# An RWKV layer with a mixture of experts: row scaling and the second layer norm on VectorE, all squares on ScalarE

## What is computed

```python
xn = layernorm(x)
# s: one RWKV layer on xn
h  = ln(xn, ln1_w, ln1_b);  xk, xv, xr = mixes of h with h shifted by one token
k, v, r = xk @ att_kw, xv @ att_vw, xr @ att_rw
x2 = xn + (sigmoid(r) * wkv(decay, first, k, v)) @ att_ow     # wkv: a scan over tokens
h  = ln(x2, ln2_w, ln2_b);  xk, xr = mixes of h with h shifted by one token
kk = square(relu(xk @ f_kw))                                  # 512 wide
s  = x2 + sigmoid(xr @ f_rw) * (kk @ f_vw)
# g: a shared expert and one of 8 routed experts a token
shared = (silu(xn @ g) * (xn @ u)) @ d
score  = sigmoid(max of the router's logits)                  # one number a token
xs     = xn * score                                           # row scaling
routed = the chosen expert's (silu(xs @ g_e) * (xs @ u_e)) @ d_e
out = x + s * silu(shared + routed)
```

## Time and profile before

| what | value |
|---|---|
| runs | 555.39, 562.61, 565.73 us (median 562.61) |
| span of the profiled execution | 552.1 us, granted clock 0.977 |
| TensorE busy | 477.2 us, 86% of the span |
| VectorE busy | 401.3 us, 73% |
| ScalarE busy | 353.4 us, 64% |
| GpSimd busy | 279.0 us, 51% |
| DMA | 64.97 MB, mean 118 GB/s |

### The profile page before, as it was taken

One profiled execution on the slowest core, in us unless ns is written; L12 is line 12 of the kernel. 1 busy time (PEld: TensorE's weight loads), 2 busy tenths in 40 slices (PEclk: granted clock), 3 DMA queues, 4 the chain that ended last, 5 costly groups with the idle time before them and its releaser, 6 DMA issues. The chain is left out here.

```text
span 552.1 us, 9051 instructions
## 1 busy us (share of the span) xinstructions
PE 477.2 (86%) x2687; PEld 356.4 (65%) x2687; DVE 401.3 (73%) x808; ACT 353.4 (64%) x707; POOL 279.0 (51%) x329
## 2 busy tenths in 40 slices
PE   1989877879998789979898989898989898869796
PEld 1989444547575556569686868686868777644454
DVE  3553697858795877858696969797878788875345
ACT  4777424656663748576878686969696968554542
POOL 7565003565756375735273737363646464634440
PEclk9999898998999999989999999999999999999799
DMA  6339508210101010126363737373737372438395
GB/s 210 102 89 248 121 0 300 108 42 13 44 20 44 1 49 12 49 55 174 114 202 111 208 106 207 101 216 94 225 100 211 102 207 92 118 115 134 69 184 109
DMA packets 62592, 64.97 MB, mean 118 GB/s; under 512 B 5776, under 2 KB 50705, under 8 KB 62496
## 3 DMA queue, kind: packets, MB, share of 16 engines
q1 hardware_dynamic: 50736, 51.16, 32.5%
q0 software_dynamic: 10656, 11.68, 9.3%
q10 hardware_dynamic: 1152, 1.56, 0.9%
HBM read 46.86 MB, written 21.12 MB: 123 GB/s over the span
## 5 line engine op out<-in xcount | busy, mean ns | idle before, releaser
L857 POOL DMA_INDIRECT routed_out<-xh,xs x71 | 91.1, 1283 | 52.5 <-ACT xh L700 34.9
L849 POOL DMA_INDIRECT tokens_by_expert<-xn,pos x64 | 70.3, 1098 | 35.1 <-issue 18.5
L471 PE MATMUL bank_ring<-xh,ew 128*128 128x128 f32 x568 | 76.8, 279 | 0.0
L471 PEld LDWEIGHTS bank_ring<-xh,ew 128*128 128x128 f32 x568 | 70.8, 194 | 4.5 <-issue 3.8
L1090 DVE TENSOR_TENSOR kk<-rk 128x512 f32<-128x512 f32 x32 | 24.2, 755 | 61.2 <-ACT rk L658 55.6
L427 PE MATMUL bank_out<-fvw,kk 128*128 128x128 f32 x512 | 67.5, 278 | 0.0
L427 PEld LDWEIGHTS bank_out<-fvw,kk 128*128 128x128 f32 x512 | 63.4, 195 | 3.9 <-issue 3.9
L692 ACT ACTIVATE px<-bank_ring 128x256 f32<-128x256 f32 x71 | 27.1, 381 | 36.7 <-PE bank_ring L471 31.3
L831 POOL TENSOR_SCALAR x_sm<-x_mv 128x4 f32<-128x4 f32 x16 | 4.0, 247 | 81.4 <-DVE x_mv L1071 81.4
L485 PE MATMUL bank_ring<-ew,hx 128*128 128x128 f32 x284 | 43.5, 276 | 0.0
L387 PE MATMUL bank_fa<-xr,att 128*128 128x512 f32 x32 | 18.3, 656 | 24.6 <-ACT rk L658 23.8
(11 more groups left out here) (143 smaller groups left out, 1145.4 us busy)
## 6 DMA issues: line engine op xcount, KB each, us to landing
ew<-ex_w SPq DMA_DIRECT2D x71, 384.0 KB
xi<-x SPq DMA_DIRECT2D x20, 256.0 KB, 2.8
tokens_by_expert<-pad_row SPq DMA_DIRECT2D x1, 4686.0 KB, 20.4
xs<-tokens_by_expert SPq DMA_DIRECT2D x71, 66.0 KB
ew<-routed_out SPq DMA_DIRECT2D x16, 256.0 KB, 3.1
out<-xn POOLq DMA_DIRECT2D x12, 256.0 KB, 6.0
routed_out<-xh,xs POOLq DMA_INDIRECT x71, 2.9
tokens_by_expert<-xn,pos POOLq DMA_INDIRECT x64
```

Of the source, the lines that this page charges most:

```text
L471: last = nc.tensor.matmul(part(GU[n % 2], q, P), part(w, q, P), xt[:, 0:P], start=True, stop=True)
L849: nc.gpsimd.indirect_dma_start(xs_dram, bass.IndirectOffsetOnAxis(ap=POS[:, t:t + 1], axis=0), XN[:, t * XROW:(t + 1) * XROW], None).then_ ...
L857: nc.gpsimd.indirect_dma_start(routed_dram, bass.IndirectOffsetOnAxis(ap=XS[(n - 2) % NXS][:, CH:CH + 1].bitcast(i32), axis=0), XH[n % NXH ...
```

## The change

The row scaling (`scale_rows`, all 71 tiles) goes from ScalarE to VectorE as a tensor_scalar with one scalar a token. z2 (`make_z2`, 64 tiles) goes from ScalarE to VectorE as a tensor_scalar that subtracts the mean and multiplies by the inverse deviation, two scalars a token; it stands behind `wkv_b`. GpSimd loses the two small instructions that made the bias (L832, L837). All four squares of the channel mix are done by ScalarE; square 1 stands between relu 2 and relu 3, and relu 3 waits for it.

```diff
-                pe.wait_ge((s_kk, s_kd)[q % 2], 2 * c + 1 + q // 2)
+                pe.wait_ge(s_kk, 4 * c + q + 1)
 ...
# ScalarE
-            def make_z2(c):
-                act.wait_ge(s_nb2, c + 1)
-                if c > 0:
-                    act.wait_ge(s_z2t, c)
-                for j in range(TPC):
-                    nc.scalar.activation(part(Z2, j, P), part(X2[c % 2], j, P), ACT.Identity,
-                                         bias=SM2[:, 2 * TPC + j:2 * TPC + j + 1],
-                                         scale=SM2[:, TPC + j:TPC + j + 1]).then_inc(s_z2, 1)
 ...
                 if c > 0 or q >= 2:
-                    act.wait_ge((s_kk, s_kd)[q % 2], 2 * c + q // 2)
+                    act.wait_ge(s_kk, 4 * c + q - 1)
 ...
-            def scale_rows(n):
-                act.wait_ge(s_xs[n % NXS], 16 * (n // NXS + 1))
-                xs = XS[n % NXS]
-                nc.scalar.activation(xs[:, 0:CH], xs[:, 0:CH], ACT.Identity, scale=xs[:, CH + 1:CH + 2])\
-                  .then_inc(s_xsc, 1)
 ...
                 if C:
                     ffn_square(i - 1, 0)
                     ffn_relu(i - 1, 2)
+                    ffn_square(i - 1, 1)
                     ffn_relu(i - 1, 3)
                     ffn_square(i - 1, 2)
+                    ffn_square(i - 1, 3)
 ...
# GpSimd, rstd_of_x2
-                nc.gpsimd.tensor_scalar(SM2[:, 2 * TPC:3 * TPC], mean, -1.0, None, ALU.mult).then_inc(s_nm2, 1)
                 pool.wait_ge(s_sm2, c + 1)
                 nc.gpsimd.tensor_tensor(SM2[:, TPC:2 * TPC], SM2[:, 0:TPC], NH[:, 0:TPC], ALU.pow).then_inc(s_rs2, 1)
-                pool.wait_ge(s_nm2, c + 1)
-                pool.wait_ge(s_rs2, c + 1)
-                nc.gpsimd.tensor_tensor(SM2[:, 2 * TPC:3 * TPC], SM2[:, 2 * TPC:3 * TPC], SM2[:, TPC:2 * TPC],
-                                        ALU.mult).then_inc(s_nb2, 1)
 ...
# VectorE
+            def make_z2(c):
+                dve.wait_ge(s_rs2, c + 1)
+                if c > 0:
+                    dve.wait_ge(s_z2t, c)
+                for j in range(TPC):
+                    nc.vector.tensor_scalar(part(Z2, j, P), part(X2[c % 2], j, P), MV2[:, 2 * j:2 * j + 1],
+                                            SM2[:, TPC + j:TPC + j + 1], ALU.subtract, ALU.mult).then_inc(s_z2, 1)
 ...
+            def scale_rows(n):
+                dve.wait_ge(s_xs[n % NXS], 16 * (n // NXS + 1))
+                xs = XS[n % NXS]
+                nc.vector.tensor_scalar(xs[:, 0:CH], xs[:, 0:CH], xs[:, CH + 1:CH + 2], None, ALU.mult).then_inc(s_xsc, 1)
 ...
                 if T:
                     wkv_b(i)
+                if C:
+                    make_z2(i - 1)
                 fill(i, 1)
 ...
                 fill(i, 7)
-                if C:
-                    ffn_square(i - 1, 1)
                 if P1:
                     running_max(i + 1)
-                if C:
-                    ffn_square(i - 1, 3)
-                if P1:
                     differences(i + 1)
```

More of the change, by code:

```diff
@@ L129, in program @@
         X2, Z2 = [sb(f"x2_{u}", CHUNK) for u in range(2)], sb("z2", CHUNK)
-        BS2, MV2, SM2 = sb("x2_bs", TPC * 6), sb("x2_mv", TPC * 2), sb("x2_sm", 3 * TPC)
+        BS2, MV2, SM2 = sb("x2_bs", TPC * 6), sb("x2_mv", TPC * 2), sb("x2_sm", 2 * TPC)
         H2 = sb("h2", BPC * (SEQ + 1))
@@ L186, in program @@
         s_sm2, s_rs2, s_z2, s_z2t = sem("x2_var_eps"), sem("x2_rstd"), sem("z2"), sem("z2_transposed")
-        s_nm2, s_nb2 = sem("x2_minus_mean"), sem("x2_minus_mean_rstd")
         s_h2, s_d2, s_mix2 = sem("h2"), sem("d2"), sem("mixed2")
-        s_fr, s_tf, s_fk, s_rk, s_kk, s_kd = (sem("fr"), sem("tanh_fr"), sem("fk"), sem("relu_fk"),
-                                               sem("kk_even"), sem("kk_odd"))
+        s_fr, s_tf, s_fk, s_rk, s_kk = sem("fr"), sem("tanh_fr"), sem("fk"), sem("relu_fk"), sem("kk")
         s_kv, s_u, s_s = sem("kv"), sem("u"), sem("s")
@@ L678, in shared_part @@
                     shared_out(m - 1)
-            def scale_rows(n):
-                act.wait_ge(s_xs[n % NXS], 16 * (n // NXS + 1))
-                xs = XS[n % NXS]
-                nc.scalar.activation(xs[:, 0:CH], xs[:, 0:CH], ACT.Identity, scale=xs[:, CH + 1:CH + 2])\
-                  .then_inc(s_xsc, 1)
             def expert_slot(n):
-                if n == -2:
-                    for t in range(3):
-                        scale_rows(t)
                 if 0 <= n < XTILES:
@@ L700, in expert_slot @@
                 nc.scalar.activation(XH[n % NXH][:, a:b], BX[:, a:b], ACT.Copy).then_inc(s_xh, 1)
-                if 3 <= n + 4 < XTILES:
-                    scale_rows(n + 4)
             def final_part(c):
@@ L727, in step @@
                 fill(i, 1)
-                if C:
-                    make_z2(i - 1)
                 fill(i, 2)
@@ L1083, in channel_mixes @@
                                                    ALU.mult, ALU.add).then_inc(s_mix2, 1)
[L1085 to L1090, removed]
             def make_s(c):
@@ L1107, in shared_part @@
                   .then_inc(s_hs, 1)
+            def scale_rows(n):
+                dve.wait_ge(s_xs[n % NXS], 16 * (n // NXS + 1))
+                xs = XS[n % NXS]
+                nc.vector.tensor_scalar(xs[:, 0:CH], xs[:, 0:CH], xs[:, CH + 1:CH + 2], None, ALU.mult).then_inc(s_xsc, 1)
             def expert_slot(n):
+                if n == -2:
+                    for t in range(3):
+                        scale_rows(t)
                 if 0 <= n < XTILES:
@@ L1115, in expert_slot @@
                       .then_inc(s_hx, 1)
+                if 3 <= n + 4 < XTILES:
+                    scale_rows(n + 4)
             def final_part(c):
```

## The result

The changed kernel takes 570.5 us (median of 4 runs, 567.3 to 572.6) where the kernel before took 561.0 beside it (4 runs, 555.4 to 565.7). The ratio is 1.028, 95% interval 1.023 to 1.034: slower. The ratio counts only runs in the faster of two states that the kernels show, and not all of those before were in it; the two medians alone would give 1.017. The forecast was 577, range 564 to 585; the profiled span was forecast at 566.8 and is 565.5 us (before 552.1).

A forecast was written before the change was run, and what follows sets the result against it. An expert step was taken as one circle through relu 3, attention_out, x2, VectorE's queue, xr2 and ffn_receptance. Eight steps at +1.5 us, +1.0, +1.3 and +0.4 gave +14.7 on a median of 562.6: 577 us, range 564 to 585.

The forecast's parts named there:

- ScalarE, relu 3: Expert step: receptance can start 0.28 us earlier, but relu 3 waits behind square 1, so attention_out stays where it was.
- px of slot 0, +0.44: Expert step, VectorE: after the earlier x2, hx of slot 0 must wait for px, losing 0.44 us.
- Four scalings at 0.21: Expert step, VectorE between x2 and xr2: four scalings add 0.84 us; the other four are hidden behind xr2.
- z2 at 0.24 a tile: Expert step, VectorE behind scan BB: four z2 tiles add 0.96 us, without waiting for GpSimd's power.
- AA no longer held, -0.73: Expert step, VectorE: with z2 ahead, scan AA starts after GpSimd's subtraction instead of beside it, gaining 0.73 us.
- z2 held off by GpSimd, +0.85: Expert step, behind BB: GpSimd's subtraction makes z2 wait about 0.85 us; the forecast's own case, 577 us, chance 0.45.
- B (slow rate): VectorE's eight chain instructions cost 0.07 us more each, without meeting GpSimd: step 28.3, kernel 575.5 us; chance 0.18.
- C (not held off): VectorE at the fast rate, z2 not held off by GpSimd: +0.72 us a step, kernel 570.6 us; chance 0.22.
- D (hidden): Something other than VectorE ends the stall before ffn_receptance, so the new work is hidden: +2.5 us, 565; chance 0.09.
- E (not slower): Gains of 0.79 and 0.73 us outweigh VectorE's eight new instructions, if under 0.135 us each: 561.7 us; chance 0.06.
- The stalls that I named as its sign: TensorE's stall before ffn_receptance grows from 0.72 to 2.2 us, and a further 0.3 stands before attention_out.
- +1.3 us from relu 3: Steps 1 to 5: relu 3 ends 0.43 us later, costing 0.26 us a step, 1.3 together.

The follow-up runs named there:

- squares only: The kernel before with only the squares moved to ScalarE, z2 and scaling as before: 571.0 us, ratio 1.029 to before.
- the table: Stretches of the expert step, start to start, for before, after, their parts and variants: steps from 26.20 to 28.52 us.
- the small subtraction: The changed kernel with GpSimd's subtraction cut to two columns of each batch from the third chunk on: 567.7 us, ratio 1.021 to before.

## Why the prediction was right, point by point

The expert step was forecast at 28.5 us and is 28.5, and its terms, measured one by one, are those of the forecast within 0.2 us each.

1. *ScalarE, relu 3.* Forecast: receptance 0.28 earlier, attention_out where it was. Measured: 0.25 less up to receptance, 0.28 more from there to attention_out. Right. It counted with the removed scaling; the experiment with the squares alone showed the second half by itself.
2. *x2 earlier by 0.79.* Measured 0.80.
3. *px of slot 0, +0.44.* hx of slot 0 starts 2.49 us after x2 (418.46 less 415.97) where it was 2.03: +0.46, after a wait of 0.37 for px. The 0.40 of "squares only" is this with a scan AA of 1.84 us in place of 1.93.
4. *Four scalings at 0.21.* Measured 0.20 each, 0.72 from x2 to xr2 in the changed kernel. Those behind xr2 are hidden, as forecast.
5. *z2 at 0.24 a tile.* Measured 0.25. All 64, with their durations (least, median, most, in ns):

```profile
L1051 DVE TENSOR_SCALAR z<-x,x_mv,x_sm x64: 314/336/1136, 102.5 to 533.9; 128x128 f32<-128x128 f32 x64
```

6. *AA no longer held, -0.73.* It takes 1.21 in place of 1.93.
7. *z2 held off by GpSimd, +0.85.* Measured 0.68, so the place is right and the size 0.17 too large: this term is the one that was mis-sized. The first z2 tile's row ends 0.09 us after L801's, so most of the tile's own 0.34 doesn't come on top of the hold. L801 ended 5.67 us after x2's start (421.64 less 415.97), where I had put it at 5.65 (412.8 less 407.15). Its durations over all steps, 1.03 to 1.99 us:

```profile
L801 POOL TENSOR_TENSOR d<-h x16: 1030/1790/1992, 52.5 to 476.8; 128x512 f32<-128x512 f32 x16
```

Rivals B (slow rate) and C (not held off) gave 28.3 and 27.7; the first fails at 0.20 us for a scaling and 0.25 for a z2 tile, the second at the 0.68 that the small subtraction gave back. D (hidden) fails: L406 follows xr2 by 0.81 us in every kernel of the table, and the step has grown with xr2. E (not slower) fails at the same prices as B. The stalls that I named as its sign are smaller, though: 0.52 before L469 and 1.35 before L406 make 1.87 where I had written 2.2 for one stall, and L394 has 0.11 in front of it where I had written 0.3. The rest of the step's growth isn't idle time: it is in the 25.0 us that TensorE's rows take in place of 24.5. The scalings beside scatters mostly kept their price (254 to 475 ns, median 278):

```profile
L1086 DVE TENSOR_SCALAR xs<-xs x71: 254/278/475, 243.2 to 479.9; 128x128 f32<-128x128 f32 x71
```

What was wrong lies outside these steps. For steps 1 to 5 I summed +1.3 us from relu 3; the traces say -2.2 up to the fifth attention_out and +4.9 for step 5, both ruled by late semaphores, which I had not read in the trace of before, though its ScalarE waited for them in steps 1, 3 and 4 (the tanh of step 4 for 1.58 us, marked "remote", at 202.80). Step 6 became 1.25 us shorter, not 1.0 longer; I didn't follow that up. These errors nearly cancel (+13.4 against +14.7), and the sum's agreement is in part luck; that of the steps is not. And the 577 for the median took over the 10.5 us by which the median of before lay above its profiled span, while the changed kernel's lies 5.0 above: that term alone is 5.5 of the 6.5 us by which I was too high.

## What to carry to other kernels

Add up a change along the circle that sets the step, start to start, and test each term there: whole times of single parts can carry events of another kind that are larger than the part (here 17 us for a part that makes the median step 0.12 us shorter). Moving work off a busy engine onto the one whose queue sets the step costs nearly its full price there (0.72 of 0.80 us for the scalings), even when both have idle time on average, and less comes back on the relieved engine (0.25). Look first at the order on the engine that releases the leader: a relu ahead of a square, for one buffer more, gave 0.8 us a step, over half of what this change lost.

## What the runs showed of the hardware

TensorE's semaphores can come up to 7.8 us after the recorded end of the products that raise them, several of them together, with ScalarE's wait often marked "remote"; in four kernels on one of three chips they never did in steps 1 to 5. In the expert steps of the kernel before, those of the down projection (L485) come up to 1.6 us late without a cost: ffn_receptance to receptance takes the same 11.18 us in kernels that don't have it.

The granted clock fell to its lower level (0.50, 1.2 GHz) for 3.4 us at the head of one expert step in seven with only the squares moved, and in three of seven in two kernels like it. Such a step took 27.6 to 28.8 us in place of 26.9.

A subtraction of GpSimd over 512 columns that is under way when a scan of VectorE ends takes 0.57 to 0.71 us from a VectorE instruction behind it, be it a scan (1.93 instead of 1.22 us), a z2 tile (1.00 instead of 0.34) or a scaling (0.84 instead of 0.27). hx, with one input from a bank, runs beside it at its usual 0.39. Where it becomes ready in the middle of the scan its own row grows too, from 1.03 to 1.99 us. The Trainium skill ("SBUF — State Buffer", Who interferes with whom) says that a VectorE instruction in a two-port mode, which tensor_scalar can enter, and GpSimd exclude each other for a whole instruction, and that one with two inputs in SBUF contends with a GpSimd instruction that reads SBUF; the rows agree with both.
